# A four-layer attention and RWKV kernel: start of the transfers, constants and the hand-written order of the steps changed together

## The reference

```python
# layer 0: x as 128 latents attends to [ctx, x]; 16 heads of 16; mask on ctx
q = x @ q_w + q_b;  k, v = split([ctx, x] @ kv_w + kv_b)
h = softmax(mask(q k / 16)) v @ out_w + out_b + x
x = gelu(rmsnorm(h) @ w1 + b1) @ w2 + b2 + x
# layer 1: 32 query heads of 8 on 8 key heads, keys and values from ctx
x = layernorm(softmax(q k / sqrt(8) + mask) v @ Wo + bo + x)
# layer 2: RWKV; token shift, low-rank mixes mw mk mv mr mg, decay w
s_new = k v^T + w s;  y = r (u k v^T + s)       # a scan over the 128 tokens
x = x + (groupnorm(y) * silu(g)) @ Wo.T;  x = x + sigmoid(fr) * (relu(fk)^2 @ fWv.T)
# layer 3: x attends to layernorm(ctx); 16 heads of 16
x = x + tanh(gate) * (softmax(q k / 4) v @ Wo.T)
```

## Time and profile before

| | us |
|---|---|
| three runs | 1128.92, 1123.29, 1126.52 |
| median of the runs | 1126.52 |
| profiled execution | 1128.1 |
| its span | 1126.1 |
| mean granted TensorE clock in it (1 is full) | 0.955 |
| PE busy | 980.3 |
| DVE busy | 806.4 |
| ACT busy | 739.1 |

### The profile page before, as it was taken

How to read it: one execution, slowest core, us unless ns; L and a number is a source line. 1 busy time by engine, 2 the same in 40 slices (tenths; PEclk the granted TensorE clock), 3 DMA queues, 4 the chain that set the end, 5 groups by cost and what they waited for, 6 DMA issues and landing times.

```text
span 1126.1 us, 23973 instructions
## 1 busy us (share of the span) xinstructions
PE 980.3 (87%) x7776; PEld 699.8 (62%) x7776; DVE 806.4 (72%) x3113; ACT 739.1 (66%) x2675; POOL 256.7 (23%) x349
## 2 busy tenths in 40 slices
PE   5779898998999899998999899998999899888356
PEld 4456566765766577665767577665766577556144
DVE  3408758886878776977878777987878776966623
ACT  1828853887658973788658983887658973881116
POOL 3102304031320413032321413031311413120300
PEclk9889999999999999999999999999999999989576
DMA  9100000000010000000010001000010000000000
GB/s 303 41 1 17 6 1 24 2 8 2 2 33 8 2 2 20 16 8 1 2 33 8 2 2 28 7 8 2 1 33 8 2 2 10 2 3 10 0 1 10
DMA packets 18091, 18.90 MB, mean 17 GB/s; under 512 B 7216, under 2 KB 16432, under 8 KB 17712
## 3 DMA queue, kind: packets, MB, share of 16 engines
q1 hardware_dynamic: 17968, 17.37, 5.1%
HBM read 15.27 MB, written 2.10 MB: 15 GB/s over the span
## 4 chain that ended last, share of the span: by engine, by line
PE 60%; DVE 14%; ACT 10%; issue 6%; POOL 2%; POOLq 0%; DVEq 0%; ACTq 0%
PE ring L678 16%; PE ring L688 15%; PE ring L730 9%; PE psS L719 5%; ACT E L1029 5%; DVE S L1213 3%; PE psO L764 2%; PE psO L772 2%; PE ring L897 2%; PE ring L669 2%; PE psO L805 2%; PE ring L887 1%; DVE slot L1389 1%; PE psS L788 1%; DVE SS L1432 1%
## 5 line engine op out<-in xcount | busy, mean ns | idle before, releaser
L1029 ACT ACTIVATE E<-S,nmax 128x128 f32<-128x128 f32 (+1 forms) x1024 | 423.7, 419 | 32.4 <-PE ring L730 21.3
L1213 DVE CUSTOM_DVE_ANT_0 S<-psS,mb 128x128 f32<-128x128 f32 (+1 forms) x1024 | 263.0, 319 | 39.8 <-ACT E L1029 17.2
L678 PE MATMUL ring<-slot,w_l 128*128 128x256 f32 x992 | 243.9, 393 | 16.5 <-ACT slot L990 12.3
L730 PE MATMUL ring<-ident,E 128*128 128x128 f32 x1280 | 202.3, 289 | 29.5 <-ACT E L1029 25.3
L678 PEld LDWEIGHTS ring<-slot,w_l 128*128 128x128 f32 x992 | 185.5, 195 | 54.8 <-ACT slot L990 14.6
L730 PEld LDWEIGHTS ring<-ident,E 128*128 128x128 f32 x1280 | 144.9, 145 | 101.8 <-ACT E L1029 63.0
L1029 ACT ACTIVATION_READ_ACCUMULATOR E<-S,nmax 128x1 f32 x1024 | 195.6, 191 | 0.0
L688 PE MATMUL ring<-w_l,slot 128*128 128x256 f32 (+1 forms) x640 | 155.1, 387 | 12.1 <-DVE slot L1453 4.7
L688 PEld LDWEIGHTS ring<-w_l,slot 128*128 128x128 f32 x640 | 116.3, 196 | 42.5 <-issue 8.8
L1016 ACT ACTIVATE ET<-ring 128x512 f32<-128x512 f32 x192 | 106.9, 587 | 17.2 <-PE ring L730 17.1
L719 PE MATMUL psS<-keys,slot 32*128 32x512 f32 (+1 forms) x768 | 97.3, 580 | 21.4 <-ACT ET L1016 12.8
(11 more groups left out here) (120 smaller groups left out, 1131.7 us busy)
## 6 DMA issues: line engine op xcount, KB each, us to landing
slot<-in_ctx SPq DMA_DIRECT2D x8, 256.0 KB, 2.8
slot<-in_x SPq DMA_DIRECT2D x8, 256.0 KB, 2.8
w_l<-in_wl SPq DMA_DIRECT2D x1, 2048.0 KB, 10.7
out<-slot SPq DMA_DIRECT2D x8, 256.0 KB, 2.1
w_l<-in_wl SPq DMA_DIRECT2D x2, 768.0 KB, 6.6
w_l<-in_wl SPq DMA_DIRECT2D x1, 1152.0 KB, 8.5
m0i<-in_m SPq DMA_DIRECT2D x8, 128.0 KB, 3.1
mb<-in_m SPq DMA_DIRECT2D x8, 128.0 KB, 2.5
```

The costliest lines, as they stand in the source:

```text
L678: m = pe.matmul(b[:, a, :], w[:, k, m0 + a * P:m0 + (a + 1) * P], src[:, k, :], start=(k == 0), stop=(k == kt - 1))
L730: m = pe.transpose(b[:, k, :], E[:, g % RING_E, k * P:(k + 1) * P], ident[:, :])
L1029: ins = act.activation(E[:, g % RING_E, h * w:(h + 1) * w], S[:, g % RING_S, h * w:(h + 1) * w], ACT.Exp, bias=nmax[:, g % 4, h:h + 1], sc ...
L1213: ins = dve.tensor_tensor_reduce(S[:, g % RING_S, h * w:(h + 1) * w], psS[g % QUAD][:, h * w:(h + 1) * w], bias[:, bb, :], -1.0, HUGE, ALU ...
```

## The change

**Transfers.** Context, X and mask of the first pair are issued first. Then come q, k, the column constants, v, two rows (`v0_b`, `v1_b`), W1 and the gate; SP then waits for v and issues the five other rows, and goes on as before. Each part has its own semaphore (`s_wq`, `s_wk`, `s_w`, `s_wv`, `s_row`, `s_rows`, `s_gate`).

**Waits.** PE waits at its start only for the identity (`s_const` 2) and for each weight part where `start` uses it. ACT and DVE wait for the columns alone. The gate's tanh stands after `aT` in `first`. `v0c`, `v0l`, `v1` of `start` wait for the zeroed buffers and the two rows; `o3` waits for the gate; `t` of `second` for the DVE constants; POOL's `sum0` of `first` for the five rows.

**Constants.** `centre`, `ones8`, `spread_j` and `gather_j` are made by a new function `constants()` that DVE calls in `cols` of `first`. `spread_j` has two parts instead of eight and takes one copy, from a new `mod32`. POOL does the small memsets first and the large buffers after.

**Bank waits.** `score_banks_free` and `output_bank_free` look up the stage ahead in a table instead of naming it by hand; they wait for the same stages where the order of stages is the same.

**Orders.** All four order texts are new. Each phase has the same steps; where they stand differs:
- `start` and `first`: `v1` ahead of `v0c`, `k1` last, of PE; `@second norm3` stands right behind `@first mask0.5` on DVE (before, behind `mask0.8`).
- In the turns: `aT` stands directly behind `yT` on PE (in `steady0` to `steady3`); `x1T` is copied ahead of it on ACT (not in `steady1` and `steady4`); `scores3.0` comes later, behind `turn0.11` to `turn0.13`; `d1` later, behind `mv`; `k1` moves behind the next phase's `scores0.0` (in `second` and `steady0` to `steady3`); DVE's `shift1` stands ahead of `mask0.12` (in `second`, `steady0`, `closing`) or of `mask0.13` (`steady1`), before it stood behind `mask0.15`; in `steady3` `v1 o1` stand ahead of `turn0.0`.
- `last`: `g2` and `bonus` move behind `vr7` on DVE; on PE `vp1` and `gather3` stand ahead of them; `fk` stands ahead of `fr` on PE and ACT.

The core of the diff:

```diff
 @block.sync
-            sp.dma_start(W0t[:, 0:qkv], wl0[:, 0:qkv]).then_inc(s_w, 16)
-            sp.dma_start(colt[:, :, :], cols).then_inc(s_w, 16)
-            sp.dma_start(rowt[:, :, :], rows.partition_broadcast(P)).then_inc(s_w, 16)
-            sp.dma_start(gate_t[:, 0:1], gate.partition_broadcast(P)).then_inc(s_w, 16)
...
             program("start", None)
+            sp.dma_start(W0t[:, 0:CT * C], wl0[:, 0:CT * C]).then_inc(s_wq, 16)
+            sp.dma_start(W0t[:, CT * C:2 * CT * C], wl0[:, CT * C:2 * CT * C]).then_inc(s_wk, 16)
+            sp.dma_start(colt[:, :, :], cols).then_inc(s_w, 16)
+            sp.dma_start(W0t[:, 2 * CT * C:qkv], wl0[:, 2 * CT * C:qkv]).then_inc(s_wv, 16)
+            for n in (ROWS.index("v0_b"), ROWS.index("v1_b")):
+                sp.dma_start(rowt[:, n:n + 1, :], rows[:, n:n + 1, :].partition_broadcast(P)).then_inc(s_row, 16)
             sp.dma_start(W1t[:, :], wl1).then_inc(s_w1, 16)
+            sp.dma_start(gate_t[:, 0:1], gate.partition_broadcast(P)).then_inc(s_gate, 16)
+            sp.wait_ge(s_wv, 16)
+            sp.dma_start(rowt[:, 1:len(ROWS) - 1, :], rows[:, 1:len(ROWS) - 1, :].partition_broadcast(P)).then_inc(s_rows, 16)
...
 @block.tensor
-            pe.wait_ge(s_setup_d, 4)
-            pe.wait_ge(s_w, WEIGHTS_IN)
+            pe.wait_ge(s_const, 2)
...
                     elif step == "q0":
                         pe.wait_ge(leaves("xT"), left("xT"))
+                        if phase == "start":
+                            pe.wait_ge(s_wq, 16)
...
 @block.scalar
-            act.wait_ge(s_w, WEIGHTS_IN)
             act.wait_ge(s_const, 3)
-            act.activation(gate_t[:, 1:2], gate_t[:, 0:1], ACT.Tanh).then_inc(s_setup, 1)
+            act.wait_ge(s_w, 16)
...
                         affine("aT", [aT[:, a, :] for a in range(CT)], col["ln3_w"], col["ln3_b"])
+                        if phase == "first":
+                            act.wait_ge(s_gate, 16)
+                            act.activation(gate_t[:, 1:2], gate_t[:, 0:1], ACT.Tanh).then_inc(s_setup, 1)
...
-            for j in range(8):
-                at = lane_at(j)
-                dve.tensor_copy(spread_j[:, j, :].rearrange("p (a b) -> p a b", b=8),
-                                ident[:, at:at + 16].unsqueeze(2).to_broadcast([P, 16, 8]))
...
-            dve.wait_ge(s_w, WEIGHTS_IN)
-            dve.wait_ge(s_setup, 1)
+            dve.wait_ge(s_w, 16)
...
+                def constants():
+
+                    dve.scalar_tensor_tensor(centre[:, :].rearrange("p (a b) -> p a b", b=16),
+                                             mod16[:, :].unsqueeze(1).to_broadcast([P, 8, 16]), -1.0 / 8,
+                                             ident[:, :].rearrange("p (a b) -> p a b", b=16), ALU.mult, ALU.add)
+                    dve.tensor_copy(ones8[:, :].rearrange("p (a b) -> p a b", b=16),
+                                    head8[:, :].unsqueeze(1).to_broadcast([P, 8, 16]))
+                    dve.tensor_copy(spread_j[:, :, :].rearrange("p a (h d) -> p (a h) d", d=8),
+                                    mod32[:, :].unsqueeze(2).to_broadcast([P, 32, 8]))
...
                     elif step == "cols":
+                        if phase == "first":
+                            constants()
```

Of the orders, the entry of PE's; the rest is as listed above:

```diff
-@start xT cT q0 k0l k0c v0c v0l k1 v1 @first scores0.0 aT turn0.0 scores0.4 turn0.1 turn0.2 turn0.3 weigh0.1 scores0.8
-weigh0.3 turn0.4 cT turn0.5 turn0.6 turn0.7 scores0.12 weigh0.5 turn0.8 turn0.9 weigh0.7 weigh0.9 turn0.10 turn0.11
+@start xT cT q0 k0l k0c v1 v0c v0l k1 @first scores0.0 aT turn0.0 scores0.4 turn0.1 turn0.2 turn0.3 weigh0.1 turn0.4
+turn0.5 scores0.8 weigh0.3 turn0.6 turn0.7 weigh0.5 turn0.8 scores0.12 cT weigh0.7 turn0.9 turn0.10 turn0.11 weigh0.9
```

More of the change, by code:

```diff
@@ L75 @@
-r2 g2 vp0 bonus nT aT u0 u1 u2 vp1 u3 cT gather3 m2 gather7 x1T yT q1 xT ynT scores1.0 q0 o2 k0l turn1.0 turn1.1
-scores1.4 weigh1.0 weigh1.1 k0c xcT turn1.2 turn1.3 scores1.8 weigh1.2 weigh1.3 v0c turn1.4 fk turn1.5 turn1.6 fr fv
-turn1.7 scores1.12 weigh1.4 turn1.8 x4T weigh1.5 turn1.9 weigh1.6 weigh1.7 weigh1.8 turn1.10 weigh1.9 q3 weigh1.10
-turn1.11 turn1.12 v0l weigh1.11 weigh1.12 turn1.13 turn1.14 k1 weigh1.13 @steady0 scores0.0 @second turn1.15 weigh1.14
-sum1 weigh1.15 v1 @steady0 turn0.0 @second o1 @steady0 turn0.1 turn0.2 scores0.4 turn0.3 weigh0.1 weigh0.3 turn0.4
@@ new lines @@
+weigh0.9 xaT k3 t turn0.11 v3 mw mk turn0.12 d1 weigh0.11 mv k2 turn0.13 turn0.14 d2 turn0.15 weigh0.13 sum0 v2
+weigh0.15 o0 mr vp0 mg r2 aT g2 bonus nT u0 u1 u2 vp1 u3 gather3 m2 gather7 x1T yT cT q1 xT ynT scores1.0 q0 o2 k0l
+turn1.0 turn1.1 scores1.4 weigh1.0 turn1.2 xcT k0c v0c scores1.8 turn1.3 weigh1.1 weigh1.2 turn1.4 fk weigh1.3 turn1.5
+turn1.6 fr fv turn1.7 weigh1.4 turn1.8 weigh1.5 scores1.12 x4T weigh1.6 turn1.9 turn1.10 weigh1.7 weigh1.8 q3 turn1.11
+weigh1.9 turn1.12 v0l turn1.13 weigh1.10 @steady0 scores0.0 @second weigh1.11 turn1.14 turn1.15 k1 weigh1.12 weigh1.13
@@ new lines @@
+turn3.5 u0 u1 u2 bonus turn3.6 weigh3.5 turn3.7 vp1 u3 weigh3.7 sum3 v3 gather3 m2 gather7 o3 yT aT x1T q1 ynT xT cT
+scores1.0 o2 q0 scores1.4 turn1.0 k0l turn1.1 turn1.2 xcT weigh1.0 k0c turn1.3 turn1.4 weigh1.1 weigh1.2 v0c scores1.8
+turn1.5 fk weigh1.3 weigh1.4 weigh1.5 turn1.6 turn1.7 fr fv weigh1.6 turn1.8 scores1.12 x4T weigh1.7 turn1.9 turn1.10
+q3 turn1.11 v0l weigh1.8 turn1.12 weigh1.9 weigh1.10 turn1.13 @steady3 scores0.0 @steady2 turn1.14 weigh1.11 weigh1.12
+weigh1.13 weigh1.14 turn1.15 k1 sum1 weigh1.15 v1 o1 @steady3 turn0.0 turn0.1 scores0.4 turn0.2 turn0.3 weigh0.1
@@ new lines @@
+scores3.4 weigh0.15 v2 turn3.1 turn3.2 r2 o0 turn3.3 g2 bonus weigh3.1 turn3.4 weigh3.3 vp0 nT turn3.5 turn3.6 u0 u1
+u2 k3 turn3.7 vp1 weigh3.5 u3 weigh3.7 sum3 v3 aT gather3 m2 gather7 o3 yT x1T q1 cT ynT scores1.0 xT o2 q0 turn1.0
+k0l turn1.1 turn1.2 scores1.4 xcT k0c turn1.3 weigh1.0 turn1.4 v0c scores1.8 weigh1.1 weigh1.2 fr turn1.5 fk weigh1.3
+turn1.6 turn1.7 weigh1.4 weigh1.5 fv turn1.8 scores1.12 x4T turn1.9 weigh1.6 turn1.10 q3 weigh1.7 turn1.11 weigh1.8
+weigh1.9 weigh1.10 turn1.12 turn1.13 v0l k1 @closing scores0.0 @steady4 turn1.14 weigh1.11 turn1.15 weigh1.12
@@ L175 @@
[L175 to L179 removed]
+exps1.15 @second exps0.0 exps0.1 exps0.2 @first sum1 @second turn0.0 turn0.1 exps0.3 turn0.2 exps0.4 exps0.5 exps0.6
@@ L242 @@
+mask1.14 turn1.10 mask1.15 turn1.11 turn1.12 turn1.13 turn1.14 @last mask3.0 mask3.1 @closing turn1.15 inv1 @last
+mask3.2 mask3.3 mask3.4 mask3.5 @closing sum1 o1 norm1 @last mask3.6 @closing apply1 @last mask3.7 @closing norm2
+@last inv3 @closing apply2 @last shift1 sum3 v3 o3 mw mk mv mr mg v2 ruk vr0 vr1 vr2 vr3 vr4 vr5 vr6 vr7 g2 bonus yT
+yn y2 o2 norm4 apply4 shift0 fv @end mask3.0 mask3.1 mask3.2 mask3.3 mask3.4 mask3.5 mask3.6 mask3.7 inv3 sum3 o3
 """
 POOL_ORDER = """
-@first norm3 sum0 scores0.0 scores0.4 scores0.8 scores0.12 @second norm3 @first scores1.0 hn x1T @second scores0.0
```

465 lines of the change are left out of this document (238 added, 227 removed).

## The result

The changed kernel takes 1146.74 us (median of four runs, 1144.78 to 1149.41) against 1127.72 of before in the same comparison (1123.29 to 1135.02): a ratio of 1.0164, with a 95% interval of 1.0103 to 1.0224. It is 19 us slower where 11 faster was forecast. The profiled execution took 1149.41, its span is 1147.4, and the granted clock's mean is 0.954 (0.955 before).

What follows compares the result with a forecast made beforehand. It saw an entry waiting for transfers, turns bound by PE with small holes, and a tail led by DVE and POOL. Terms -3.5, -6 and -1.6 sum to -11.1, taking 1126.5 to 1115 us; 8-in-10 range 1102 to 1128.

Steps and rivals of the forecast that it cites:

- Change 1: Entry: the new transfer order starts q0 near 7.1 instead of 12.78, -5.7 us, bounds -4.6 and -6.6.
- Change 2: Second's norm3 placed earlier: DVE stands 6.0 us for the context, leaving -3.5 of the entry's gain.
- Change 3: Steps placed anew in the turns: -6 us, bounds -20 and +12.
- PE work put in is work taken from elsewhere: Layer 0's attention is ACT's time: +6.4 of PE work moves in, ACT's content grows 3.0, net -3.4.
- scores3.0's wait: PE's 2.1 us wait ahead of layer 3's first scores, partly covered by turn-overs: 0.3 a turn, -1.8.
- x1T's term: x1T copied ahead of aT shrinks q1's wait from 1.7 to about 0.7, but it moves to ynT: 0.
- The factor of three quarters: Scaling of the turns' summed gain of -8.2 to -6, as a filled hole often opens the next.
- Change 4: Last turn: g2 and bonus leave the scan chain, fk goes ahead of fr: -1.6 us, bounds 0 and -2.5.
- Rival 2: Slower, 1138.3: earlier shift1 delays masks (6.8), plus ACT's 3.0, o1's hold and like spells (5.1); chance 0.10.
- Rival 1: Turns gain nothing as holes only move: 1121.4, no measurable change; chance 0.28 with its neighbourhood.
- Rival 3: Larger gain: no stand at norm3 and 3 us less idle in each of six turns, 1101.2; chance 0.20 with all below 1108.
- Rival 4: Entry's gain lost in full: PE idles, its clock falls at scores0.8 too: 1119.4; within the forecast's 0.42.

Runs made afterwards that it cites:

- e12: Changed kernel with second's norm3 on DVE back behind mask0.8 instead of mask0.5: 1147.08 us, ratio 1.0163 to the kernel before.
- e2: As e1, but with the new orders up to steady0's first scores and the old from there: 1133.46 us, ratio 1.0051.
- e1: Changed kernel (new transfers, waits, constants) with all four order texts of before: 1124.85 us, ratio 0.9964 to the kernel before.
- e17: As e1, with steady0's turn and steady2's layer 0 stretch and middle new, but steady2's r2 to gather3 steps in former order: steady2's piece costs 2.3 us.
- e5: As e1, with PE's scores3.0 moved from behind turn0.10 to behind turn0.12 in six turns: 1124.82 us, ratio 0.9966.
- e8: As e1, with PE's d1 moved behind mv in steady0 to closing: 1129.04 us, ratio 0.9994.
- e7: As e1, with k1 moved behind weigh1.15 on PE and behind sum1 on ACT in five turns: 1130.73 us, ratio 1.0008.
- e6: As e1, with ACT copying x1T ahead of aT in steady0 to closing: 1125.49 us, ratio 0.9966.
- e11: As e1, with the new orders from layer 2 of last on, those of end included: 1121.97 us, ratio 0.9948.
- e9: Changed kernel with DVE's steps where first meets second (turn1.14, mask0.0, inv1, turn1.15) placed as before: 1148.15 us, ratio 1.0169.

## Why the prediction was wrong

**Change 1 (-5.7 at q0): right in kind, mis-sized.** It was -2.3. The term of 0.9 for 384 KB more in the queue should have been 3.1: the columns landed at 8.5, not at 6.3, beyond the bound of 7.4. And the table load was not at 0 but at its bound of 1.28, ahead of the copy of xT. "ACT waits for the columns" was in the text, and that it would load its table only after that wait was not drawn from it. X's transposes were at 4.43, as forecast.

**Change 2 (2.2 of the entry lost at norm3): the stand was there, its price was smaller.** 3.62 in the trace, forecast 6.0. By e12 and e2 it costs 0.7, at most 1.7, and the times don't show it. The sum for both changes was -3.5; e1 has -2.0 to -2.4 by its trace. The slow matmuls that a rule of the Trainium skill (TensorE: Matmul & The Clock Gate, The HAM clock gate) would put behind the stand are there from 36 to 42 us in the changed kernel, and as many in e1, which has no stand (the changed kernel first, then e1; the clock is third from last):

```profile
36.00:42.00 6.00, 5.35 (x52) 3.25 (x52) 3.43 (x20) 4.58 (x16) 1.04 (x1) 0.72 0.01 1
```

```profile
36.00:42.00 6.00, 4.66 (x35) 2.32 (x36) 4.53 (x21) 5.03 (x18) 1.75 (x2) 0.73 0.00 1
```

**Change 3 (-6): wrong, and the cause of nearly the whole miss.** Measured +24.6 from first's m2 to closing's scores1.0. The step that failed is "PE work put in is work taken from elsewhere", with its net of -3.4. The first half was right in sum: over six turns layer 0's stretch took 4.7 of PE work (forecast 6.4), grew by 1.9 (forecast 3.0) and lost 2.8 of idle time (forecast 3.4). Turn by turn it was not: in steady3 2.0 of work went in and the stretch grew by 3.4. The second half took for granted that the middle and layer 1's stretch are PE's own time, so that they shorten by what leaves them and stay tight in any order. Newly placed, they have 11.6 and 4.5 more idle, 4.4 and 2.1 of it in steady2. For the middle of steady2 it is shown that the sequence does most of it (e17 has 2.8 of 4.2 back at yT); that the other turns and layer 1's stretch go the same way is likely and not shown. A part of the 24.6 is not idle time: between these two steps PE's idle time grew by 20.6 and its busy time by 4.0, with seven spells at half clock where the kernel before has four. I had listed the holes that the new order fills and never asked for the ones that it opens.

The other terms of change 3 were measured singly, and none is a gain: scores3.0's wait (-1.8) gives way to one at turn0.11 (e5); d1's (-3.0, though five turns at 0.5 are 2.5) moves to mv (e8); k1 put later costs (e7). Only x1T's term, put at 0 because its wait would move, was right, though it moved to cT and a transfer (e6) in the old order, and to ynT (1.89) in the new. The factor of three quarters for "a filled hole often opens the next" was far too high: in the old order none of the three fillings brought anything.

**Change 4 (-1.6): right up to q3, not shown to the end.** From t to yT 43.1 became 41.7, from there to q3 32.5 became 32.0: -1.9; e11 -1.5 to -2.1. From q3 to o3 the changed kernel takes 1.5 longer (e11 1.3), 1.0 of it at q3 under the half clock, so its trace keeps 0.4 of the gain and e11's 0.8. The two ratios, 0.9948 and 0.9964, allow 1.6 as well as 0.

**The rivals.** Rival 2 forecast slower, 1138.3, at a chance of 0.10. Its sign came true. Its mechanism can't be the main one: steady2 and steady3 lose 5.8 and 5.7 with shift1 in its old place. It is not excluded in `second`, which loses most (7.3). There shift1 moved from ahead of mask0.15 to ahead of mask0.13 (not mask0.12), and t waits for its product, as it does not in e1; no run moves shift1 alone:

```profile
145.16 2.08 PE L912 MATMUL ring<-slot,w_l 128*128 128x256 f32 x8 [1.50 <-DVE slot L1421]
```

Rival 2's loosest part, a spell of waiting in the other turns, was nearest the truth, and was put at 5.1. Rival 1 ("holes only move") was right for every single step and wrong for the whole. The range's upper end of 1128 stood on it; the bound of +12 that the text itself gave for change 3 led to 1133, and was left out of the range. That bound was too low by the text's own rival 2, which came to 16.9, and the measured 24.6 lies beyond both.

Rival 3 needed no stand at norm3, and there was one. Rival 4's fall of the clock is there (at 37.2, in scores0.8), but the kernel before and e1 have theirs at 41.1 and 38.8, in scores0.12, so it cost nothing new.

**Still open.** The 7.0 of `second` (e2) are shown to be its order's, but not by which steps; the one that I named was not it (e9). In steady3 and steady4 the middle was not divided as in steady2, and layer 1's stretch in none.

## What to carry to other kernels

A wait in an order-by-hand pipeline belongs to the chain that is late, not to the step that meets it: look at what the code makes the step wait for (the profile's releaser is only inferred), move something in that engine's list, or expect the wait at the next step. Count what an order opens as well as what it fills: a stretch in which PE never waits can be tight by its alternation of products from different chains, and then sorting them by kind costs there (2.8 us in the one turn where it was tried). Try a new order of one turn alone between old ones before it goes into all; here that read prices of up to 7.6 us out of one profile, fine to about 1.5, once the granted clock of both traces is compared over the same steps.
